# The output of a transformer block stored by 32 indirect transfers of GpSimd instead of eight plain ones of SyncE

## The reference

```python
x = x + 0.5 * ffn(layernorm(x), Wr, W1, W2)
x = x + attn(layernorm(x), qkv_w, qkv_b, out_w, out_b)
x = x + 0.5 * ffn(layernorm(x), Wr, W1, W2)
```

## Time and profile before

| | |
|---|---|
| median of 3 runs | 1371.33 us (1371.33 to 1372.31) |
| the profiled execution | 1371.65 us, its span 1369.9 us |
| TensorE busy | 1254.1 us, 92% |
| VectorE busy | 1134.6 us, 83% |
| ScalarE busy | 801.9 us, 59% |
| GpSimd busy | 153.7 us, 11% |
| mean granted TensorE clock | 0.989 of full speed |
| the eight stores of the output | 256 KB each, median 2.4 us from issue to landing |

### The profile page before, as it was taken

How to read it: one execution, slowest core, us unless ns; L and a number is a source line. 1 busy time by engine, 2 the same in 40 slices (tenths; PEclk the granted TensorE clock), 3 DMA queues, 4 the chain that set the end, 5 groups by cost and what they waited for, 6 DMA issues and landing times.

```text
span 1369.9 us, 27688 instructions
## 1 busy us (share of the span) xinstructions
PE 1254.1 (92%) x8192; PEld 596.7 (44%) x8192; DVE 1134.6 (83%) x2314; ACT 801.9 (59%) x1540; POOL 153.7 (11%) x458
## 2 busy tenths in 40 slices
PE   5999999999798888888888888888889899999998
PEld 3766666666312222222222222222222576767776
DVE  7877877788799999899988998899896687777775
ACT  4433333333268888888888888888888323333332
POOL 1022012221211111111111111111111000000000
PEclk9999999999879999999999999999999999999999
DMA  7010011110311111111111111111111211101100
GB/s 200 1 47 24 25 47 46 47 28 20 86 44 55 42 41 41 54 41 41 41 54 41 41 41 54 41 41 41 50 49 49 61 35 34 35 14 29 32 1 16
DMA packets 52135, 59.19 MB, mean 43 GB/s; under 512 B 10977, under 2 KB 33377, under 8 KB 52065
## 3 DMA queue, kind: packets, MB, share of 16 engines
q1 hardware_dynamic: 52064, 58.36, 14.2%
HBM read 26.22 MB, written 31.72 MB: 42 GB/s over the span
## 4 chain that ended last, share of the span: by engine, by line
PE 74%; ACT 12%; DVE 6%; issue 6%; DMA 1%; ACTq 1%; DVEq 0%; SPq 0%
PE ps L779 21%; PE ps L921 19%; PE ps L766 14%; PE ps L907 14%; ACT probs L675 12%; PE ps L736 2%; DVE X L1106 1%; PE ps L756 1%; DVE act L1094 1%; PE ps L700 1%; DVE mx L1252 1%; ACTq L78 1%; PE ps L743 1%; PE ps L773 0%; PE ps L878 0%
## 5 line engine op out<-in xcount | busy, mean ns | idle before, releaser
L1252 DVE TENSOR_REDUCE mx<-ps 128x1 f32<-128x1024 f32 x512 | 608.3, 1220 | 65.0 <-PE ps L878 44.8
L675 ACT ACTIVATE probs<-ps 128x512 f32<-128x512 f32 x1024 | 534.5, 601 | 106.9 <-PE ps L907 106.9
L907 PE MATMUL ps<-Q,K 51*128 51x512 bf16 x1024 | 310.9, 384 | 55.4 <-ACT probs L675 55.2
L604 ACT ACTIVATE sg<-ps,unscale 128x512 f32<-128x512 f32 x256 | 173.8, 687 | 312.1 <-PE ps L779 276.3
L878 PE MATMUL ps<-K,Q 48*128 48x512 bf16 x1008 | 339.7, 389 | 4.6 <-DVE mx L1252 3.6
L921 PE MATMUL ps<-probs,vh 128*32 128x512 f32 x2048 | 273.9, 607 | 0.1
L766 PEld LDWEIGHTS ps<-w,act 128*128 128x128 f32 x2048 | 247.9, 192 | 17.1
L766 PE MATMUL ps<-w,act 128*128 128x128 f32 x2048 | 249.0, 275 | 0.0
L907 PEld LDWEIGHTS ps<-Q,K 51*128 51x128 bf16 x1024 | 80.3, 93 | 362.4 <-ACT probs L675 328.2
L1094 DVE SCALAR_TENSOR_TENSOR act<-ps,unscale,sg 128x512 f32<-128x512 f32 x256 | 183.1, 744 | 58.5 <-PE ps L779 17.9
L779 PE MATMUL ps<-x_hi,w_hi 128*128 128x512 f16 x512 | 194.7, 380 | 13.2 <-DVE act L1094 8.5
(11 more groups left out here) (86 smaller groups left out, 605.1 us busy)
## 6 DMA issues: line engine op xcount, KB each, us to landing
o_parts<-ot SPq DMA_DIRECT2D x64, 256.0 KB, 2.2
q_stack<-parts SPq DMA_DIRECT2D x48, 128.0 KB, 2.3
k_stack<-parts SPq DMA_DIRECT2D x48, 128.0 KB, 2.3
Q<-q_stack SPq DMA_DIRECT2D x64, 96.0 KB, 2.3
K<-k_stack SPq DMA_DIRECT2D x64, 96.0 KB, 2.3
att<-o_parts SPq DMA_DIRECT2D x16, 256.0 KB, 3.6
probs<-w_in SPq DMA_DIRECT2D x8, 256.0 KB, 5.0
rden<-rdens SPq DMA_DIRECT2D x8, 256.0 KB, 4.2
```

The lines of the kernel that those rows point to most:

```text
L604: nc.scalar.activation(sg[:, j, :], hid[2 * j], ACT.Silu, scale=unscale[:, e, 2 + j:3 + j]).then_inc(silu_done, 1)
L675: nc.scalar.activation(probs[:, kb % PSLOTS, j * CH:(j + 1) * CH], score[i], ACT.Exp, scale=SCALE).then_inc(probs_ready, 1)
L907: nc.tensor.matmul(score[i], K[u][0:ROWS, kb * P:(kb + 1) * P], Q[u][0:ROWS, j * CH:(j + 1) * CH], start=True, stop=True).then_inc(scores_ ...
L1252: nc.vector.tensor_reduce(mx[:, u % 2, t:t + 1], pair.rearrange("p a b -> p (a b)"), AX_X, ALU.max).then_inc(max_read, 1)
```

## The change

The eight `store_out` transfers and the last wait go from SP's queue. POOL gets a table `row_id[128, 32]` of unsigned integers, filled once by an iota with `row_id[p, t] = 128*t + p`. For each chunk, POOL waits for the same count of `acc_done` and issues four indirect transfers, one for each tile of 128 rows: row p of the tile is written to row `row_id[p, t]` of `out`. POOL's loop over `sum_attention` is written out so that the sum of chunk c+2 is ahead of the stores of chunk c, and POOL waits at the end for all 32.

```diff
+        row_id = sb("row_id", [P, N // P], U32)
...
-            def store_out(c):
-                sp.wait_ge(acc_done, E * (NCH + c + 1))
-                row = c * CH
-                sp.dma_start(out[bass.ds(row, CH), :].rearrange("(t p) d -> p t d", p=P),
-                             X[:, bass.ds(c * TPC, TPC), :]).then_inc(out_stored, 16)
-
...
-                store_out(CPB * r + u)
...
-            for u in range(CPB):
-                tail(NCH // CPB - 1, u, att_ahead=False, den_ahead=False)
-            sp.wait_ge(out_stored, 16 * NCH)
...
+            seq.then(nc.gpsimd.iota(row_id[:], pattern=[[P, N // P]], base=0, channel_multiplier=1))
...
-            with pool.Fori(1, NCH // CPB) as r:
-                for u in range(CPB):
-                    sum_attention(r, u)
+
+            def store_rows(c):
+
+                pool.wait_ge(acc_done, E * (NCH + c + 1))
+                for t in range(TPC * c, TPC * (c + 1)):
+                    nc.gpsimd.indirect_dma_start(out, bass.IndirectOffsetOnAxis(ap=row_id[:, t:t + 1], axis=0),
+                                                 X[:, t, :], None).then_inc(out_stored, 16)
+
+            for c in range(NCH):
+                if c + 2 < NCH:
+                    sum_attention((c + 2) // CPB, c % CPB)
+                store_rows(c)
+            pool.wait_ge(out_stored, 16 * TPC * NCH)
```

## The result

| | before | changed |
|---|---|---|
| median of 5 runs | 1371.33 us | 1378.8 us (1377.25 to 1380.3) |
| ratio | | 1.005, 95% interval 1.0036 to 1.0065 |
| the profiled execution | 1371.65 us, span 1369.9 | 1378.38 us, span 1376.6 |
| from the end of VectorE's last addition to the end of the span | 2.8 us | 9.4 us |

The kernel is slower, as forecast, but by 7.5 us where 3.9 were forecast. The time lies in the range (1372.6 to 1380.3), though outside the 1374.2 to 1377.4 that the forecast had by itself. Nearly the whole loss of the profiled execution is behind the last arithmetic: 9.4 - 2.8 = 6.6 us of the 6.7 by which the span grew.

What follows compares the result with a forecast made beforehand. TensorE's own stream was taken to set the pace, only the last store being on the path. Four issues of 1.27 us plus 1.58 us after 1367.15, against 1369.9, gave +3.9: 1371.33 + 3.9 = 1375.2 us, range 1372.6 to 1380.3.

Steps and rivals of the forecast that it cites:

- The direction and the place: Slower, +3.9 us, all behind VectorE's last addition; slower by over 0.2% was given 0.72.
- The seven groups at 0: Indirect POOL stores of the first seven chunks, under matmuls: covered by POOL's idleness, costed at 0.
- The time of one issue: One indirect store issued on POOL: 1.27 us, taken from `att_sum`; four in series at the end, 5.08 us.
- What comes after the last issue: From the fourth POOL issue to the end of the span: 0.52 + 1.05/4 + 0.35 + 0.45 = 1.58 us.
- the 0.45: Time in us between the old SP store's landing and the span's end, carried over to the new end.
- its own signs: Right: last addition near 1367.1, POOL transfers 1.0 to 1.8 us apart, then about 1.6 us. Wrong: unnamed POOL work.
- the dear issue: Rival at the end: each indirect store costs two POOL additions, 2.54 us; +9.0 us, 1380.3 us; chance 0.13.
- Cheap issue: Rival at the end: POOL issues the four stores quickly, 0.7 us each giving +1.6, 1373.0 us; chance 0.25.
- the deciding 0.98: Time in us per POOL issue below which the change stays under 2.74 us, about 0.2%, not told from nothing.
- g: Time of issuing one indirect store on POOL; the change at the end is 4g - 1.17 us.
- Collision: Rival at the seven hidden groups: 28 issues hold up VectorE and delay TensorE by 10.1 us; 1385.3 us; chance 0.06.
- Faster: Rival: SP's freed queue or smaller transfers remove TensorE's stalls; at most -1.8 us, 1369.5 us; chance 0.03.

Runs made afterwards that it cites:

- experiment 4: Changed kernel with the seven hidden chunks stored by SP's plain transfers, only the last by four indirect POOL stores; 1377.62 us, ratio 1.0037 to the kernel before.
- experiment 1: Changed kernel with the last chunk stored by one plain SP transfer, the other seven groups still on POOL; 1371.33 us, ratio 1.0001 to the kernel before.
- experiment 8: Changed kernel with one more drain on POOL after the seventh group of stores; 1376.35 us, ratio 1.0025 to the kernel before.
- experiment 7: Changed kernel with all eight chunks stored by one plain 256 KB POOL transfer each; 1373.6 us, ratio 1.0005 to the kernel before.
- experiment 3: Changed kernel with the last chunk stored by one plain 256 KB POOL transfer instead of four indirect ones; 1374.99 us, ratio 1.0028 to the kernel before.

## Why the prediction was right, and what it lacked

**The direction and the place: right.** The loss lies behind the last addition, and the middle has not moved: the last addition is 0.05 us later, TensorE's waits are 2.1 us against 2.2. SP's seven stores were worth nothing: with them back on SP (experiment 4), TensorE's waits are 1.6 us, which is within the scatter.

**The seven groups at 0: wrong at the close.** Their issues are hidden, and experiment 1, which keeps exactly those, is at 1.0001. But each of the 28 transfers adds 0.082 us to POOL's closing drain, 2.3 us in all, and in the changed kernel this drain is on the path. Without them (experiment 4) or with their share drained early (experiment 8) the tail is 7.3 us (0.23 of it for a longer first issue) and 7.1 us instead of 9.4. Had only the last group's four transfers been in the drain (0.40 us), the forecast's tail of 6.7 us would have been short by about 0.4.

**The time of one issue: right.** I took 1.27 us from POOL's two-operand addition; it is 1.26 from start to start. That it matched an addition was luck: it is 0.96 us of work and 0.30 until the next, and no run shows a mechanism that the two share. A plain transfer of 512 rows is issued in 0.75 to 0.82 us (once 0.96, the first of experiment 7's program), so the rows alone do not make the price; no run varied the rows of an indirect one. Four issues with the start behind the addition (0.27) take 1372.20 - 1367.18 = 5.02 us, forecast 5.08.

**What comes after the last issue: one term missing.** The forecast put 1.58 us behind the fourth issue, taken apart from the old store: first packet 0.52, data 0.26, landing 0.35, and 0.45 "for the final wait and what closes the program". Measured are 1376.6 - 1372.20 = 4.4. Without the drain of 2.69 it would be 1.7, so the four terms held together to 0.1 us. The step that failed is the last of them, the 0.45: the close was taken from an end in which SP came last, and with the final wait moved to POOL it is POOL's close that counts. It has a drain of 0.075 us plus 0.082 for each of POOL's transfers that no earlier drain has cleared, 2.3 us of it for the groups that were costed at 0. Sum: 5.02 + 1.7 + 2.69 = 9.4 us, against 2.8 before. By its own signs the prediction fails here: it asked for about 1.6 us behind the last issue, and it calls itself wrong if POOL does something after its last transfer that the text does not name. It gave this no price. The time lies in its range only because the range reaches up to the dear issue, which did not occur; that part is luck.

**The rivals.** *Cheap issue* fell: 1.26 us is over the deciding 0.98, and doubling the last group added 5.1 us (14.8 - 9.4 = 5.4, less 0.33 of drain). The Trainium skill says that many descriptors can be generated before the added cost shows ("DMA: Bandwidth & Descriptors", section "Anatomy of one DMA — SWDGE (gpsimd) path"). The rival stretched this from the descriptors of one transfer to four transfers, and these did not overlap on POOL. For one plain transfer the trace does not speak against it: 512 rows in 0.82 us. The same page (section "Latency and other measured facts") has the first byte of a GpSimd transfer at about 1 us and that of one from SP at 0.6, 0.4 apart. Counted from the start of the issue, the first packets came here after 1.5 us (indirect, 1371.24 to 1372.77), 1.4 (POOL's plain one in experiment 3, 1366.90 to 1368.30) and 0.9 (SP, 1367.15 to 1368.05): the difference is near the page's, 0.5 to 0.6, and the times themselves are longer. Behind the end of the issue it is 0.57 us, where the forecast had 0.52, so this difference is already in the issue's own length.

*Dear issue* fell as a mechanism (g = 2.54, measured 1.26), but its time, 1380.3, is nearer to the measured 1378.8 than the forecast's 1375.2. Whoever reads the time alone would have picked it; the spacing of the issues rules it out. *Collision*: no sign in the changed kernel, 2.1 us of waits against 2.2. *Faster*: not seen.

**What stays open.** Ratio and medians put the loss at 4.9 to 8.9 us, the profile at 6.7. Where the last addition falls in an execution, 1366.6 to 1370.5 us, differs by more than some of these effects, in the kernel before too by its runs; no run looked for the reason. Why a drain costs 0.082 us per transfer was not tried either. Whether an indirect issue goes with its rows is open. And whether the 1.0 us of TensorE's waits with 56 hidden issues is a collision or scatter is not settled.

## What to carry to other kernels

A transfer's price at the end of a program is the issue, the landing and the close of the engine that issued it, and on POOL this close counts the earlier transfers too: keep the final store on an engine whose close is cheap, or let the engine drain earlier, where it is idle. When a last step moves to another engine, read that engine's closing instructions in the trace and do not carry over the old engine's remainder. Use POOL's indirect transfers where the rows are really irregular, and then as far from the end as possible: each is 1.26 us of POOL in series. Hidden ones were free here but for their 0.082 us each in the drain, which is paid if POOL is the last to close.

## What the runs showed of the hardware

- With POOL idle ahead of it, its drain takes 0.075 us plus 0.0816 us for each transfer that POOL has issued since the last drain, indirect (64 KB) or plain (256 KB), and long after most of them have landed: 0.402 us (4 transfers), 0.727 (8 plain ones), 2.362 (28), 2.443 (29), 2.688 (32), 3.015 (36), 4.977 (60). An earlier drain takes the account with it: 0.381 with 4 since then. A drain that starts while POOL works ends later by that: 2.815 with 32 and a mark (2.70 behind the mark), 1.234 beside an `att_sum` and no transfers (0.07 behind it).
- An indirect store of 128 rows takes POOL 0.96 us with 0.30 until the next can start, in series of four and of eight alike. A plain one of 512 rows takes 0.75 to 0.82, the first of a program 0.96. The first indirect one of a program took 1.19, and the fourth of the changed kernel 1.49, for which no run looked for a reason.
- POOL's transfers leave in larger packets than SP's: 64 KB of rows of 512 B went out as 16 packets of 2 to 8 KB and 16 of under 512 B, in some 0.25 us, where SP's 256 KB took 512 packets of under 2 KB and 16 small ones.
